# Output chunks of a fused mixture-of-experts and recurrence kernel: two halves of four consecutive steps in place of odd and even steps

## The chip, the cores and the metric

The kernel runs on one core of a Trainium2 chip. The metric is the device time in microseconds of one execution, as the median of several runs. Engines are named as in the profile: PE is the matrix engine (PEld its weight loads), DVE the vector engine, ACT the scalar engine, POOL the GpSimd engine, SP the engine that here only issues DMAs; SPq, PEq and so on are the instruction queues of these engines.

## The reference, cut to what matters

The input x is 32 sequences of 256 steps of 256 channels. First a mixture-of-experts layer is added to it (8192 tokens, a shared gated network and the two best of 8 experts each). Its result is called x again, and a recurrence over the 256 steps is added:

```
x = x + moe(x, cond)
def step(h, z_t):
    gate = sigmoid(h @ Wh.T + z_t @ Wz.T + b)
    h_new = tanh(h * (1 - alpha) + gate * z_t)
    return h_new, h_new
out = x + scan(step, cond, x over the 256 steps)
```

So each output value is one element of the recurrence's input plus the state of that step. The states follow one another: step s needs the state of step s-1.

## The kernel before, in words

All work of the mixture layer is cut into 170 numbered units (152 of experts and of the shared network, then 18 drain units), each a fixed sequence of PE instructions with numbered gaps between them. The recurrence runs beside it: one step is 12 small matmuls on PE (`gate_high`, `gate_step`), a tanh on ACT (`act_gate`, L1241), two DVE operations (`rec_pre`: `taken` L1542, `pre` L1545), two tanh on ACT (`act_h`: `hs_high` L1249, `hist` L1250) and two more DVE operations (`rec_low`: `hs_low` L1551, and `kept` L1534 for the step after). In which gap of which unit each piece of a step stands is written out by hand in the tables `PE_AT`, `ACT_AT` and `DVE_AT`; every engine runs its instructions strictly in that order, with semaphores between the engines.

On chip the channels are on the 128 partitions, in two halves (`KC = 2`), and within a partition the steps and the 32 sequences (`NB = 32`) follow one another. `zq` holds the recurrence's input halved, `hist` the states of the last 24 steps, both with the 32 sequences contiguous and the steps 64 elements apart.

The output leaves in 32 chunks of 8 steps (`HALF = 8`), at the units of the table `OUT_AT` (46 to 156). A chunk goes through four engines:

- `out_channels(c)` on DVE (L1565) computes 2 * zq + hist for 8 steps and 32 sequences, 256 elements per partition, once for each of the two channel halves, into the tile `o_ch` (64 instructions in all). Between the two there is a gap in which pieces of recurrence steps may stand.
- PE (L1922), one unit later, turns `o_ch` with four transposes of 128 x 128 into the PSUM bank `spare`: two token groups of 128 tokens, two channel halves.
- ACT (`act_out`, L1184) copies the bank to `o_tok`, of which there are two. Chunk c may overwrite what chunk c-2 used once its store has landed (L1183).
- SP (`store`, L958-959) waits for the copy and issues one DMA of 256 KB to the output in DRAM.

The 8 steps are numbered t * 2 + j. A token group is one j: group 0 has the even steps, group 1 the odd ones, and a partition of `o_tok` is one (sequence, t) and holds the rows of both j, which are neighbours in DRAM, so each partition is stored as one run of 2 KB. For that, `o_ch` is laid out as (j, sequence, t) with t innermost, four values:

```
out_v = out.rearrange("b (a t j) c -> a b t (j c)", t=TT, j=2)            # L532
o_ch[:, kc].rearrange("p j b t -> p t j b")                               # L1565, the output
```

The inner loop of the DVE instruction runs over the 32 sequences, and so writes with a stride of four elements (16 bytes); both of its inputs are read in runs of 32 neighbouring elements.

SP issues in program order, unit by unit (`body`): the load of the residual, the transposing loads of token pairs for the experts (`load_pair`, L948), the stores of expert results (`store_pair`, L967), transposing loads of tokens (`turn_x`, L928) and plain ones (`load_x`, L912), then the output store of that unit (L959), and last, at section borders, the first loads of the next section (`first_pairs`). At the very end it waits until all stores have landed (L1018-1019). The expert results stored by SP are read back by indirect DMAs of POOL (L1121) and summed on DVE (`gated`, L1506 and L1510).

Of the kernel before, what the change touches and what calls it, by code (L numbers as in the profile page):

```python
# [13 lines left out]
P = 128  # L14
# [484 lines left out]
def moe_gated_recurrence(nc, x, cond, router_w, router_b, w1, w3, w2, w1e, w2e, gate_w, gate_b, alpha, out):  # L499
    NB, T, C = x.shape  # L500
    E, _, HE = w1e.shape
    HS = w1.shape[1]
    KC = C // P
    TT = P // NB
# [3 lines left out]
    HALF = TG // 2  # L508
# [4 lines left out]
    NSTEP = T  # L513
# [15 lines left out]
    x_slots = [nc.dram_tensor(f"x_slots_{n}", [NT * P, 2 * C], F16).ap() for n in ("even", "odd")]  # L529
    y_slots = [nc.dram_tensor(f"y_slots_{n}", [NT * P, C], F32).ap() for n in ("even", "odd")]  # L530
    x_in = x.rearrange("b (q t j) c -> q b t (j c)", t=TT, j=GROUP)
    out_v = out.rearrange("b (a t j) c -> a b t (j c)", t=TT, j=2)  # L532

    with ExitStack() as ctx:
        def sb(name, shape, dt=F32):
            return ctx.enter_context(nc.sbuf_tensor(name, shape, dt))

        def sem(name):
            return ctx.enter_context(nc.semaphore(name))
# [112 lines left out]
        hist = sb("hist", [P, TS, KC, NB])  # L652
        hs = [sb(f"hs_{h}", [P, 2, KC, NB], F16) for h in HL]
        th = sb("th", [P, 2, KC, NB])
        pre = sb("pre", [P, 2, KC, NB])
        o_ch = sb("o_ch", [P, KC, 2, NB, TT])
        o_tok = sb("o_tok", [P, 2, 2, C])


# [70 lines left out]
        s_out = [sem(f"s_out{i}") for i in range(4)]  # L730
# [17 lines left out]
        def released(eng, what, part):  # L748

            at = SPARE.index((what, part))  # L750
            if at == 0:
                return
            what, part = SPARE[at - 1]
            if what == OUT:
                eng.wait_ge(s_otok, part + 1)
            elif what == LOGITS:
                eng.wait_ge(s_lg, part + 1)
            elif what == SUM:
                eng.wait_ge(s_z, part[0] * KC + part[1] + 1)
            else:  # L760
                eng.wait_ge(s_rk, part + 1)

        def turned(eng, q):

            if q < N_TURN:
                eng.wait_ge(s_xslo, KC * (q + 1))
            else:
                eng.wait_ge(s_xs[q % NXP], len(range(q, N_TURN - 1, -NXP)) * (16 * GROUP))
# [82 lines left out]
        def conv_parts(key):  # L851

            kind, i = key
            if kind == "w1e":
                k, m = divmod(i, 2)
                src = w1e[:, k * P:(k + 1) * P, m * P:(m + 1) * P].rearrange("e p h -> p e h")
                return src, [w[k][m][:].rearrange("p e h -> p (e h)") for w in w1e_s], 1, E, P
            if kind == "w2e":
                k, part = divmod(i, 2)
                some = slice(part * (E // 2), (part + 1) * (E // 2))  # L860
                src = w2e[some, k * P:(k + 1) * P, :].rearrange("e p c -> p e c")
                return src, [w[k][:, some].rearrange("p e c -> p (e c)") for w in w2e_s], 1, E // 2, C
            if kind == "w13":
                src, dst = (w1, w3)[i].rearrange("(k p) h -> p k h", p=P), [w[:, i] for w in w13_s]
                return src, [d.rearrange("p k h -> p (k h)") for d in dst], 1, KC, HS
            src, dst = w2.rearrange("(k p) h -> p k h", p=P), [w[:, :, :] for w in w2_s]
            return src, [d.rearrange("p k h -> p (k h)") for d in dst], 1, MID, C
# [31 lines left out]
        def z_of(c):  # L899

            return zq[:, c // 2 % NZQ, (c % 2) * HALF:(c % 2 + 1) * HALF]
# [5 lines left out]
        def _(sp):  # L907
# [48 lines left out]

            def store(c):
                sp.wait_ge(s_otok, c + 1)  # L958
                sp.dma_start(out_v[c], o_tok[:, c % 2].rearrange("p j c -> p (j c)")).then_inc(s_out[c % 4], 16)  # L959

            def store_pair(u):

# [53 lines left out]
            for u in UNITS:  # L1016
                body(u)
            for part in range(4):  # L1018
                sp.wait_ge(s_out[part], 16 * (NSTEP // HALF // 4))


        @block.gpsimd
# [122 lines left out]
        def _(act):  # L1145
# [7 lines left out]
            for n in range(N_ACT_LOADS):  # L1153
                src, _, a, k, w = conv_parts(CONV[n])
# [24 lines left out]
            def act_out(c):  # L1179
                act.wait_ge(s_turno, c + 1)  # L1180

                if c >= 2:
                    act.wait_ge(s_out[(c - 2) % 4], ((c - 2) // 4 + 1) * 16)  # L1183
                nc.scalar.activation(o_tok[:, c % 2].rearrange("p j c -> p (j c)"),  # L1184
                                     spare[:], ACT.Copy).then_inc(s_otok, 1)

# [70 lines left out]
            def body(u):  # L1257
# [41 lines left out]
                if MISC.get(u.i, (None,))[0] == OUT:  # L1299
                    act_out(MISC[u.i][1])  # L1300
# [50 lines left out]
        def _(dve):  # L1351
# [204 lines left out]
            def out_channels(c, gap):  # L1556

                dve.wait_ge(s_h, (c + 1) * HALF + 1)
                if c > 0:
                    dve.wait_ge(s_turno, c)  # L1560
                some = slice(c * HALF % TS, c * HALF % TS + HALF)
                for kc in range(KC):
                    if kc > 0:
                        gap()
                    ins = dve.scalar_tensor_tensor(o_ch[:, kc].rearrange("p j b t -> p t j b"),  # L1565
                                                   z_of(c)[:, :, kc, :].rearrange("p (t j) b -> p t j b", j=2), 2.0,
                                                   hist[:, some, kc, :].rearrange("p (t j) b -> p t j b", j=2),
                                                   ALU.mult, ALU.add)
                ins.then_inc(s_och, 1)

# [126 lines left out]
            for t in range(TT):  # L1697
                ins = dve.tensor_copy(cond_t[:, :, :, t], bank[0][:, 0:COLS].rearrange("p (k b) -> p k b", k=KC))
# [20 lines left out]
        def _(pe):  # L1719
            PASSES = ((0, 0), (1, 0), (0, 1))  # L1720

            def mm(out_ap, w, mov, start, stop):
                return pe.matmul(out_ap, w, mov, start=start, stop=stop, skip_group_check=True)  # L1723

            def pairs(out_ap, w, mov, start, stop, chunks):


                last, n = None, len(chunks) * 3
                for i, k in enumerate(chunks):
                    for j, (a, c) in enumerate(((0, 0), (1, 0), (0, 1))):  # L1730
                        last = mm(out_ap, w(a, k), mov(c, k), start and i == 0 and j == 0, stop and i * 3 + j == n - 1)
                return last
# [117 lines left out]
            def sum_routed(q, kc, gap):  # L1850

                for j in range(GROUP):
                    if j > 0:
                        gap()
                    if kc == 0:
                        pe.wait_ge(s_r, q * GROUP + j + 1)
                    last = pe.transpose(spare[:, j * P:(j + 1) * P], r_sum[:, j, kc * P:(kc + 1) * P], ident[:])  # L1857
                last.then_inc(s_half if kc == 0 else s_y, 1)
# [36 lines left out]
            def misc(what, part, gap):  # L1895
                released(pe, what, part)
                if what == LOGITS:
                    for q in range(TILE0[part] // GROUP, TILE0[part + 1] // GROUP):
                        turned(pe, q)
                    for j in range(SECTIONS[part]):  # L1900
                        q, i = divmod(TILE0[part] + j, GROUP)
                        last = pairs(spare[:, j * E:(j + 1) * E],
                                     lambda a, k: xs[:, q % NXS, a, k, i * P:(i + 1) * P],
                                     lambda c, k: rwx[c][:, k, :], True, True, range(KC))
                    last.then_inc(s_lgps, 1)
                elif what == RANKS:
                    J = SECTIONS[part]
                    pe.wait_ge(s_route, part * N_ROUTE_LINKS + MASK_LINK)
                    chosen = mask16[:, 0:J].rearrange("p j e -> p (j e)")
                    mm(spare[:, 0:J * E], below[:], chosen, True, False)  # L1910
                    for d in range(1, J):
                        mm(spare[:, d * E:J * E], ones16[:], chosen[:, 0:(J - d) * E], False, False)
                    for j in range(J):
                        last = mm(spare[:, J * E:J * E + E], ones16[:], mask16[:, j, :], False, j == J - 1)
                    last.then_inc(s_rkps, 1)
                elif what == SUM:
                    sum_routed(*part, gap)
                else:
                    pe.wait_ge(s_och, part + 1)
                    for j in range(2):  # L1920
                        for kc in range(KC):
                            last = pe.transpose(spare[:, j * C + kc * P:j * C + (kc + 1) * P],  # L1922
                                                o_ch[:, kc, j].rearrange("p b t -> p (b t)"),
                                                ident[:])
                    last.then_inc(s_turno, 1)

# [109 lines left out]
```

## Time and profile before

| | before |
|---|---|
| median of 3 runs | 783.67 us (783.11 to 784.78) |
| profiled execution | 779.37 us |
| its span, first to last instruction | 777.3 us |
| mean granted TensorE clock | 0.959 |
| PE busy | 714.0 us, 92% |
| DVE busy | 548.3 us, 71% |
| ACT busy | 472.2 us, 61% |
| DMA packets | 167106, 124.83 MB |

The profiled execution is one run with the hardware profiler on. Its span leaves out 2.1 us of start and end that its own time has. Busy is the time in which an engine works on an instruction; the chain that ended last is followed back from the last instruction, at each step to what released it. A granted clock of 1.0 is the full clock of PE, 0.5 half of it. In the windows below, the number in brackets behind a busy time is the count of instructions; the last three are the granted clock, the mean busy share of the DMA engines, and the GB/s they moved.

### The profile page before, as it was taken

How to read it: one execution, taken by the hardware profiler on the slowest of the kernel's cores; microseconds unless marked ns; L12 is line 12 of the kernel's file. 1: busy time of each engine (PE TensorE's matmuls, PEld its weight loads, DVE VectorE, ACT ScalarE, POOL GpSimd, SP SyncE). 2: the span in 40 equal slices, each digit the busy share in tenths (PEclk: the TensorE clock that was granted, in tenths of full speed). 3: DMA queues.
4: the chain of work that ended last, by engine and by line, in shares of the span. 5: the costliest groups of instructions: out<-in, count | busy, mean ns of one | idle time of the engine just before them, and what ended most of it. 6: DMA issues, size and time to landing. Idle time of an engine off the chain costs nothing.

```text
span 777.3 us, 23838 instructions
## 1 busy us (share of the span) xinstructions
PE 714.0 (92%) x8562; PEld 513.2 (66%) x8562; DVE 548.3 (71%) x2014; ACT 472.2 (61%) x1347; POOL 269.7 (35%) x284
## 2 busy tenths in 40 slices
PE   5899998988999899999989999999999999999763
PEld 3455486544888656898658887566888655686442
DVE  4887651437877498876658987798885678866754
ACT  4745574624677565667647676565877645676533
POOL 2037365155642056453066015774030073002100
PEclk9999999989999999999989999999999999999865
DMA  8836799683896767887949854456476355123101
GB/s 287 312 115 230 211 232 284 170 198 106 199 252 160 172 114 190 184 207 168 189 142 217 173 125 157 137 164 144 104 180 162 103 145 141 43 89 117 43 14 42
DMA packets 167106, 124.83 MB, mean 161 GB/s; under 512 B 119346, under 2 KB 147796, under 8 KB 166996
## 3 DMA queue, kind: packets, MB, share of 16 engines
q1 hardware_dynamic: 151076, 79.20, 42.7%
q0 software_dynamic: 14368, 41.96, 18.2%
q10 hardware_dynamic: 1552, 2.15, 0.8%
q8 instruction: 76, 1.25, 0.7%
q14 instruction: 34, 0.28, 0.1%
HBM read 39.90 MB, written 55.84 MB: 123 GB/s over the span
## 4 chain that ended last, share of the span: by engine, by line
PE 70%; DVE 13%; ACT 6%; DMA 4%; issue 3%; SPq 2%; DVEq 0%; ACTq 0%; POOL 0%; POOLq 0%
PE bank L1723 66%; PE bank L1922 2%; PE bank L1857 2%; SPq L928 2%; DVE hid_low L1491 1%; DVE pre L1545 1%; DMA xe<-x_slots_even 1%; DVE full L1484 1%; DVE taken L1542 1%; ACT th L1241 1%; ACT hs_high L1249 1%; DMA xs<-x_parts 1%; DVE r_part L1506 1%; DVE r_sum L1510 1%; DVE o_ch L1565 1%
## 5 line engine op out<-in xcount | busy, mean ns | idle before, releaser
L1723 PE MATMUL bank<-xe,w1e_high 128*128 128x128 f16 x1360 | 216.8, 221 | 5.9 <-DMA xe<-x_slots_even 3.9
L1723 PE MATMUL bank<-xs,w_high 128*128 128x512 f16 x512 | 169.4, 386 | 5.0 <-DVE w_low L1661 2.8
L1723 PE MATMUL bank<-xe,w1e_low 128*128 128x128 f16 x680 | 147.8, 220 | 0.0
L1491 DVE TENSOR_TENSOR hid_low<-full,hid_high 128x512 f16<-128x512 f32 (+1 forms) x152 | 103.0, 677 | 46.6 <-ACT hid_high L1194 36.6
L1723 PEld LDWEIGHTS bank<-xe,w1e_high 128*128 x1360 | 115.3, 98 | 26.3 <-issue 13.8
L1241 ACT ACTIVATE th<-bank 128x64 f32<-128x64 f32 x256 | 56.9, 222 | 104.6 <-PE bank L1723 100.5
L1542 DVE SCALAR_TENSOR_TENSOR taken<-th,zq 128x64 f32<-128x64 f32 x256 | 57.8, 226 | 79.9 <-ACT th L1241 75.8
L1249 ACT ACTIVATE hs_high<-pre 128x64 f16<-128x64 f32 x256 | 65.5, 256 | 72.2 <-DVE pre L1545 63.3
L1723 PEld LDWEIGHTS bank<-hs_high,gwt_high 128*128 128x128 f16 x1024 | 70.1, 97 | 49.5 <-ACT hs_high L1249 34.3
L1062 POOL TENSOR_TENSOR fence_pool<-zero 128x1 f32<-128x1 f32 x12 | 2.9, 245 | 282.2 <-DMA y_slots_odd<-y_pair 88.4
L1723 PE MATMUL bank<-xs,w_low 128*128 128x512 f16 x256 | 98.8, 386 | 0.0
L1723 PE MATMUL bank<-hs_high,gwt_high 128*128 128x32 f16 x1024 | 79.0, 178 | 20.3 <-ACT hs_high L1249 20.0
L1723 PE MATMUL bank<-w2e_high,hid_high 128*128 x340 | 93.2, 274 | 0.4 <-ACT y_pair L1203 0.3
L1723 PE MATMUL bank<-w2e_low,hid_high 128*128 x340 | 92.5, 272 | 0.0
L1723 PE MATMUL bank<-w2e_high,hid_low 128*128 x340 | 92.2, 271 | 0.0
L1103 POOL DMA_INDIRECT x_slots_even<-x_parts,where x72 | 76.2, 1059 | 44.4 <-PE bank L1723 32.9
L1723 PEld LDWEIGHTS bank<-xs,w_high 128*128 128x128 f16 x512 | 49.7, 99 | 57.8 <-issue 10.1
L1121 POOL DMA_INDIRECT y_got<-y_slots_even,where x72 | 72.2, 1003 | 39.1 <-PE bank L1723 22.1
L1551 DVE TENSOR_TENSOR hs_low<-hist,hs_high 128x64 f16<-128x64 f32 x256 | 56.6, 221 | 37.2 <-ACT hist L1250 34.8
L1723 PE MATMUL bank<-hs_high,gwt_low 128*128 128x32 f16 x1024 | 77.6, 177 | 0.0
L1103 POOL DMA_INDIRECT x_slots_odd<-x_parts,where x56 | 57.0, 1018 | 48.9 <-PE bank L1723 41.8
L1723 PE MATMUL bank<-hs_low,gwt_high 128*128 128x32 f16 x1024 | 66.2, 179 | 5.2 <-DVE hs_low L1551 4.0
(156 smaller groups left out, 1709.3 us busy)
## 6 DMA issues: line engine op xcount, KB each, us to landing
y_slots_even<-y_pair SPq DMA_DIRECT2D x45, 256.0 KB
y_slots_odd<-y_pair SPq DMA_DIRECT2D x37, 256.0 KB
x_res<-in_x_dram SPq DMA_DIRECT2D x16, 512.0 KB
out_dram<-o_tok SPq DMA_DIRECT2D x32, 256.0 KB, 3.1
x_tok<-in_x_dram SPq DMA_DIRECT2D x14, 512.0 KB, 4.5
x_slots_even<-zeros POOLq DMA_DIRECT2D x1, 4096.0 KB, 17.9
x_slots_odd<-zeros POOLq DMA_DIRECT2D x1, 4096.0 KB, 15.2
y_got<-in_L_cond_W1e_dram SPq DMA_DIRECT2D x4, 512.0 KB, 11.2
```

The source lines that it names most:

```text
L928: sp.dma_start_transpose(xs[:, q % NXS].rearrange("p h k s -> p (h k) s")[:, :, j * P:(j + 1) * P], halves(q)[:, j].rearrange("p h c -> p ...
L1103: pool.indirect_dma_start(x_slots[n % 2], at_slots(n, j, k), halves(q)[:, i].rearrange("p h c -> p (h c)"), None).then_inc(s_scat[n % 2], 16)
L1121: pool.indirect_dma_start(y_got[:, tile % NYG, k, :], None, y_slots[n % 2][0:(2 * PAIRS[n] - 1) * P, :], at_slots(n, j, k)).then_inc(s_got ...
L1241: nc.scalar.activation(flat3(th[:, s % 2]), gate_sums(s), ACT.Tanh, scale=0.5 / UP).then_inc(s_th, 1)
L1249: nc.scalar.activation(flat3(hs[0][:, s % 2]), src, ACT.Tanh).then_inc(s_hhi, 1)
L1484: dve.scalar_tensor_tensor(buf, buf, 1.0 / UP, shared_bank(u, 1)[:], ALU.mult, ALU.mult).then_inc(s_prod, 1)
L1491: dve.tensor_tensor(hid[1][:, u.i % NR, some], full32[:, u.i % 2, some], hid[0][:, u.i % NR, some], ALU.subtract).then_inc(s_lo, 1)
L1542: dve.scalar_tensor_tensor(flat3(taken[:, s % 2]), flat3(th[:, s % 2]), 1.0, flat3(z_of(s // HALF)[:, s % HALF]), ALU.add, ALU.mult).then_ ...
L1551: dve.tensor_tensor(flat3(hs[1][:, s % 2]), flat3(hist[:, s % TS]), flat3(hs[0][:, s % 2]), ALU.subtract).then_inc(s_hlo, 1)
L1723: return pe.matmul(out_ap, w, mov, start=start, stop=stop, skip_group_check=True)
L1857: last = pe.transpose(spare[:, j * P:(j + 1) * P], r_sum[:, j, kc * P:(kc + 1) * P], ident[:])
L1922: last = pe.transpose(spare[:, j * C + kc * P:j * C + (kc + 1) * P], o_ch[:, kc, j].rearrange("p b t -> p (b t)"), ident[:])
```

## The change

An output chunk keeps its 8 steps, but they are split as first four, last four, not as even and odd. `o_ch` becomes (step, sequence), so the sum is written without a stride, and with plain contiguous runs; the four transposes read halves of it, in which a partition of the result is one (t, sequence). A partition of `o_tok` then has two rows that are four steps apart, so each half is stored by a DMA of its own, 128 KB, each partition one run of 1 KB. The semaphores of the stores count 32 for a chunk where they counted 16. The order tables are untouched.

```diff
-    out_v = out.rearrange("b (a t j) c -> a b t (j c)", t=TT, j=2)
+    out_v = out.rearrange("b (a t) c -> a t b c", t=TT)
...
-        o_ch = sb("o_ch", [P, KC, 2, NB, TT])
+        o_ch = sb("o_ch", [P, KC, HALF, NB])
...
             def store(c):
                 sp.wait_ge(s_otok, c + 1)
-                sp.dma_start(out_v[c], o_tok[:, c % 2].rearrange("p j c -> p (j c)")).then_inc(s_out[c % 4], 16)
+                for j in range(2):
+                    sp.dma_start(out_v[2 * c + j], o_tok[:, c % 2, j]).then_inc(s_out[c % 4], 16)
...
             for part in range(4):
-                sp.wait_ge(s_out[part], 16 * (NSTEP // HALF // 4))
+                sp.wait_ge(s_out[part], 32 * (NSTEP // HALF // 4))
...
                 if c >= 2:
-                    act.wait_ge(s_out[(c - 2) % 4], ((c - 2) // 4 + 1) * 16)
+                    act.wait_ge(s_out[(c - 2) % 4], ((c - 2) // 4 + 1) * 32)
...
-                    ins = dve.scalar_tensor_tensor(o_ch[:, kc].rearrange("p j b t -> p t j b"),
-                                                   z_of(c)[:, :, kc, :].rearrange("p (t j) b -> p t j b", j=2), 2.0,
-                                                   hist[:, some, kc, :].rearrange("p (t j) b -> p t j b", j=2),
+                    ins = dve.scalar_tensor_tensor(o_ch[:, kc], z_of(c)[:, :, kc, :], 2.0, hist[:, some, kc, :],
                                                    ALU.mult, ALU.add)
...
                             last = pe.transpose(spare[:, j * C + kc * P:j * C + (kc + 1) * P],
-                                                o_ch[:, kc, j].rearrange("p b t -> p (b t)"),
+                                                o_ch[:, kc, j * TT:(j + 1) * TT].rearrange("p t b -> p (t b)"),
                                                 ident[:])
```

## Rows read from the trace of the kernel before

**Rows 1.** Windows: stretch, length, busy us of PE, PEld, DVE, ACT, POOL, clock, DMA.
```profile
222.00:745.00 523.00, 503.63 (x6595) 375.65 (x6593) 396.67 (x1504) 341.07 (x1075) 172.36 (x179) 0.98 0.60 145
745.00:777.30 32.30, 13.39 (x191) 9.39 (x190) 14.79 (x65) 11.38 (x49) 0.00 (x0) 0.60 0.09 34
```

**Rows 2.** Waits of PE, 222 to 745 us: total us, times, longest.
```profile
PE bank L1723 <- ACT hs_high L1249: 7.3, 10, 1.3
PE bank L1723 <- DVE hs_low L1551: 4.0, 5, 2.8
...
PE bank L1922 <- DVE o_ch L1565: 0.4, 1, 0.4
```

**Rows 3.** Page, part 4: the chain that ended last, shares of the span.
```profile
PE 70%; DVE 13%; ACT 6%; DMA 4%; issue 3%; SPq 2%; DVEq 0%; ACTq 0%; POOL 0%; POOLq 0%
```

**Rows 4.** The chain in order of time: start us, length us, what.
```profile
292.24 0.40 DVE r_sum L1510
...
293.24 1.01 DVE o_ch L1565 x2
...
750.09 0.52 DVE o_ch L1565
```

**Rows 5.** DVE groups by shape: count, busy us, mean ns, idle before.
```profile
L1491 DVE TENSOR_TENSOR hid_low<-full,hid_high 128x256 f16<-128x256 f32 x6 | 2.5, 420 | 0.4 <-ACT hid_high L1194 0.4
L1506 DVE SCALAR_TENSOR_TENSOR r_part<-y_got,gate,x_res 128x256 f32<-128x256 f32 x64 | 30.5, 477 | 3.4 <-DMA y_got<-y_slots_even,where 3.4
L1524 DVE SCALAR_TENSOR_TENSOR zq<-bank,zq 128x512 f32<-128x512 f32 x32 | 21.9, 684 | 2.4 <-PE bank L1857 2.2
L1565 DVE SCALAR_TENSOR_TENSOR o_ch<-zq,hist 128x256 f32<-128x256 f32 x64 | 38.5, 620 | 0.5 <-ACT hist L1250 0.5
L1698 DVE COPY cond_t<-bank 128x64 f32<-128x64 f32 x4 | 0.7, 261 | 1.8 <-PE bank L1995 1.8
L1473 DVE COPY ranks<-bank 128x104 f32<-128x104 f32 x5 | 1.3, 258 | 0.0
L1473 DVE COPY ranks<-bank 128x40 f32<-128x40 f32 x1 | 0.2, 190 | 0.0
```

**Rows 6.** The output store's line: issue ns min/median/max, then landing.
```profile
L959 SPq DMA_DIRECT2D out_dram<-o_tok x32: 539/605/1508, 228.4 to 774.4; - x32
DMA to landing us min/median/max: 2.3/3.1/4.5
```

**Rows 7.** Timeline of SP around 380 us, merged: start, length.
```profile
379.44 0.61 SPq L959 DMA_DIRECT2D out_dram<-o_tok  x1
380.14 6.45 SPq L948 DMA_TRANSPOSE xe<-x_slots_odd  x4
```

**Rows 8.** The chain in the same stretch, in order of time.
```profile
383.07 0.72 SPq L948
...
385.29 1.30 SPq L948
...
387.27 4.16 DMA y_slots_even<-y_pair
```

**Rows 9.** The chain's end, in order of time.
```profile
771.49 0.61 DVE o_ch L1565
772.70 1.10 PE bank L1922 x4
...
773.83 0.60 ACT o_tok L1184
```

**Rows 10.** Timeline of SP at the end: start, length.
```profile
774.45 0.54 SPq L959 DMA_DIRECT2D out_dram<-o_tok  x1
```

**Rows 11.** Waits of SP's queue, 774 us to the end: total us, times, longest.
```profile
SPq L1019 <- DMA out_dram<-o_tok: 1.7, 1, 1.7
```

**Rows 12.** DMA view, 774 us to the end: rates in 40 slices, then all packets.
```profile
GB/s 0 0 0 0 0 0 0 0 0 0 0 0 0 0 0 0 0 0 0 25 273 472 447 397 422 397 397 273 75 0 0 0 0 0 0 0 0 0 0 0
DMA packets 144, 0.26 MB, mean 79 GB/s; under 512 B 16, under 2 KB 16, under 8 KB 144
```

## The prediction

> **What bounds the kernel now.** I read the windows first, then what PE waits for, then the chain, then the groups of DVE by shape. From 222 us, when the first chunk leaves, to 745 us PE is busy 503.6 of 523 us [rows 1]: the reader is to see that nothing that shortens another engine can win more than the 19.4 us that are left, and that DVE at 396.7 us has much slack on average. What PE waits for by name in there is small: 7.3 us for `hs_high`, 4.0 us for `hs_low`, both steps of the recurrence, and 0.4 us for `o_ch` itself [rows 2]. After 745 us only the recurrence is left: PE busy 13.4 of 32.3 us, at a mean granted clock of 0.60, so a part of the time at 1.2 GHz [rows 1]. There the loop PE, ACT, DVE, ACT sets the time. The chain is PE for 70% of the span, DVE for 13%, SP's queue for 2% [rows 3], so both engines that the change touches do stand on it, in places.
>
> **The sum on DVE.** The stride is what the change removes, so what does it cost? L1565 takes 620 ns for 256 elements [rows 5]. Two other two-input operations on 256 elements are contiguous at the output: `hid_low` 420 ns, which writes fp16, and `r_part`, which reads a scalar per partition as well, 477 ns. A second estimate is of the stride alone: L1698 is a copy of 64 elements from PSUM which writes with this same stride of four floats, 261 ns; the copies L1473 of 40 and 104 elements without it take 190 and 258 ns, so 64 elements would take 190 + 24/64 * 68 = 215 ns. The stride costs 46 ns for 64 elements, or 0.7 ns each, 180 ns for 256. That brings 620 to 440 ns, between the two. Reading with a stride is not the cost: L1524 reads PSUM with a stride of four floats and writes runs of 32, and takes 684 ns for 512 elements. I take 420 ns, because `hid_low` has no scalar operand and neither has L1565; the bounds are 620 (no gain) and 420, and 477 lies between. In the chain, where each piece ends when the next instruction starts, `r_sum` holds DVE for 0.40 us and a pair of `o_ch` for 1.01 us [rows 4]; a pair at 420 ns is about 0.6 to 0.7 us. So each of the 64 instructions frees 0.20 us, 12.8 us of DVE's busy time.
>
> The Trainium skill speaks against this gain: its page "SBUF — State Buffer", section "Door 1: The DMA port swizzle", says that SBUF is reached in lines of 16 bytes, that an access to a new line pays, and that fp32 can be strided by 4 for free. The stride here is 4, so by that limit L1565 would stay at 620 ns and the sum would be the third rival's. The trace differs, with the 0.7 ns an element above.
>
> **What of it lies on the path.** 12.8 us less of DVE is not 12.8 us of time. On the chain before the last chunk I count eight pieces of `o_ch` with nine instructions in all, of which rows 4 show the first, a pair at 293.24, and the last, at 750.09. That last one gives nothing: the tanh that the next DVE operation needs is itself only just done. That leaves eight instructions, 8 * 0.20 = 1.6 us, if nothing else comes in their place. But PE has the next claim: in these stretches it is nearly full and its own order is fixed, and the named wait for `o_ch` is 0.4 us in all [rows 2]. I take half, 0.8 us, with 0 and 1.6 as bounds. For the other 50 or so instructions PE's work is the cover; were the cover gone, they would be worth at most 0.2 us each.
>
> **The tail.** The last chunk stands wholly on the chain: the pair starts at 771.49, PE's transposes at 772.70, ACT's copy at 773.83 [rows 9], SP's issue at 774.45 [rows 10]. The pair is 0.4 us shorter (0.28 at 477 ns, 0 if the stride is free). Transposes and copy have the same shapes as before: nothing.
>
> **The stores.** Each chunk has one DMA issue more on SP. An issue takes 0.605 us at the median, 0.54 at least [rows 6]. In all 32 * 0.6 = 19 us of SP's queue, and most of it beside SP's waits for ACT, PE and DVE. The packets cost little: of a run of 2 KB two of 1 KB are made, 4096 packets more, of the same bytes.
>
> Behind the store in the queue stand the loads of token pairs. One place is on the chain: the store at 379.44 has four loads behind it [rows 7], the third of which waits on PE and goes at 383.07, then an expert store lands after 4.16 us [rows 8], and POOL's gather and DVE's sum wait for that. Two loads at about 1.3 us each [rows 8] after 380.14 are out by 382.74, so 0.33 us before 383.07. A second issue of 0.65 us uses that up and makes this stretch 0.32 us later, if the gather's delay reaches PE. I take 0.3 us; bounds 0 and 0.65. The wait for `o_tok` on chunk c-2 (L1183) asks for a landing of 3.1 us, 4.5 at most [rows 6], of a store several units back: nothing. The thresholds of 32 need both halves, which follow each other by one issue.
>
> At the end, SP issues at 774.45 for 0.54 us and waits 1.7 us more for the landing [rows 10, 11]. The data moves in nine of 40 slices of 3.3 us, 0.75 us for 0.26 MB [rows 12], so a half takes 0.37 us. After the change the first half leaves with the same first issue; the second is issued 0.54 + 0.05 us later and lands its 0.37 us of data behind that. 0.59 + 0.37 - 0.75 = 0.2 us later than before. The trace shows no output store of 128 KB; if an issue has the 0.605 us median and the landing does not shrink with the size, it is 0.65 us later; if the second issue is cheaper than the first, 0. I take 0.2.
>
> **The sum**, against the profiled execution's own 779.37 us: - 0.8 (middle) - 0.4 (last pair) + 0.3 (SP at 380 us) + 0.2 (last landing) = - 0.7 us, so 778.7 us. The median of the runs shown is 783.67, 4.3 us above that execution; I take the difference over unchanged: 783.67 - 0.7 = 783.0 us. The bounds of the terms give - 0.4 - 1.6 = - 2.0 us, and + 0.65 + 0.65 = + 1.3 us.
>
> **Rivals.**
> First, more than the chain shows: the recurrence runs ahead. A shorter `o_ch` lets every step behind it finish earlier, and PE's waits for `hs_high` and `hs_low`, 11.3 us in the middle [rows 2], shrink. For it speaks that the tables put pieces of steps right behind `o_ch`; against it, that PE waits on these in 15 places only, while there are 32 chunks, and that the gaps' order is fixed, so a step that is ready early waits for its gap. If a third of these waits goes, 3.8 us, with the last pair 4.2 us, less the 0.5 of the stores: 780.0 us. Half of that effect already leaves my band: 781.9 us.
>
> Second, the stores cost more than the sum gives: slower. The mechanism is SP's queue: with the transposing loads at 1.3 us each and issues at 0.6 us, a section's start is a train without gaps, and 0.65 us put into it moves every load behind. It decides from the point where the slack ahead of SP's next wait is under 0.65 us; at 380 us it is 0.33. The price is 0.65 us for each train that a store meets; if four of the 32 chunks meet one on PE's path, 2.6 us, and with 0.65 at the end and 0.4 won by the last pair: + 2.85 us, 786.5 us; with two, 785.2. Against it speaks that SP's queue has 2% of the chain [rows 3], and most of that before the first store.
>
> Third, the change does not do what it says: L1565 stays near 620 ns since the cost is in reading two SBUF inputs in runs of 32 elements, and not in writing. Then only the stores' + 0.5 us are left, 784.2 us, 1.2 us more at most. L1698 speaks against it. This is where the Trainium skill's limit, cited above from "SBUF — State Buffer", would lead.
>
> **How the numbers follow.** What a measurement of this kernel can tell from no change is about 0.2%, 1.6 us: faster is below 782.1, slower above 785.2. My forecast, 783.0 us, has a chance of 50%, the recurrence that runs ahead 22%, the queue 20%, the stride that costs nothing 8%. Of the forecast 5 points are faster and 45 the same; of the first rival 20 and 2; of the second 16 points are slower and 4 the same; the 8 are the same. That is 0.25 faster, 0.59 same, 0.16 slower. The forecast alone ranges from 781.7 to 785.0 us. The range for 8 in 10 reaches towards both other cases: 780.6 to 785.9 us.
>
> **What would show it.** L1565 at 400 to 480 ns, with DVE's busy time 9 to 13 us lower; 64 issues of L959 and 4096 packets more, and some 500 of 4 bytes for semaphores; `taken` and `hs_low` behind a lone `o_ch` start 0.2 us earlier but PE's waits in the middle stay within 1 us of 11.7; the last pair to the transposes 0.8 us in place of 1.21; the last landing wait about as now but behind a second issue. It would be wrong if L1565 stays above 550 ns, if PE's idle time in the middle falls by more than 2 us, or if the waits for DMAs of `xe` or `y_got` grow by more than 1 us.

## The result, and the profile after

The change makes the kernel slower: 789.71 us (787.38 to 792.86, 9 runs) against 783.11 us (778.91 to 786.75, 9 runs) for the kernel before, a ratio of 1.0096 with a 95% interval of 1.007 to 1.0123 (the ratio compares all runs of the two kernels; their two medians alone give 1.0084). The forecast was 783.0 us, 0.1% under the 783.67 us that were known for the kernel before, with a range up to 785.9 us. The profiled execution took 789.71 us, its span is 787.9 us, 10.6 us more than before.

The groups of DVE by shape come first, as in rows 5: count, busy us, mean ns, idle before.

```profile
L1507 DVE SCALAR_TENSOR_TENSOR r_part<-y_got,gate,x_res 128x256 f32<-128x256 f32 x64 | 30.6, 479 | 8.3 <-DMA y_got<-y_slots_even,where 7.0 <-issue 1.3
L1566 DVE SCALAR_TENSOR_TENSOR o_ch<-zq,hist 128x256 f32<-128x256 f32 x64 | 26.3, 420 | 0.5 <-ACT hist L1251 0.5
```

The sum does what it was to do: 420 ns in place of 620 [rows 5]. But the other row has changed too: `r_part` waits 7.0 us for gathered expert results, where it waited 3.4 [rows 5]. The time did not go to DVE's work.

The windows of the same two stretches, as in rows 1:

```profile
222.00:745.00 523.00, 497.75 (x6502) 370.36 (x6500) 382.36 (x1480) 337.75 (x1061) 174.22 (x178) 0.98 0.66 145
745.00:787.90 42.90, 19.93 (x260) 14.16 (x260) 19.34 (x86) 14.75 (x62) 0.00 (x0) 0.59 0.08 25
```

In the middle PE is busy 5.9 us less in the same 523 us, so it waits more, at the same clock. The mean busy share of the 16 DMA engines is 0.66 and was 0.60, while they move the same 145 GB/s [rows 1]. The DMA engines are busy longer for the same bytes: that is the first sign.

PE's waits from 222 to 745 us, as in rows 2:

```profile
PE bank L1722 <- ACT hs_high L1250: 7.7, 9, 1.3
PE bank L1722 <- DVE hs_low L1552: 6.6, 5, 5.5
PE bank L1722 <- issue: 4.0, 7, 1.4
```

The wait of 5.5 us ends at 400.65 us. It is the wait that was the longest in rows 2 too, with 2.8 us. The chain before it, in order of time (start us, length us), and SP's timeline (start, length, merged) say what grew:

```profile
388.37 2.11 SPq L948
...
391.29 3.44 DMA y_slots_even<-y_pair
...
396.97 2.87 DMA y_got<-y_slots_even,where
...
399.97 0.48 DVE r_part L1507
400.45 0.15 DVE hs_low L1552
```

```profile
379.95 1.25 SPq L960 DMA_DIRECT2D out_dram<-o_tok  x2
381.32 9.16 SPq L948 DMA_TRANSPOSE xe<-x_slots_odd  x4
```

This is the place that the prediction looked at in rows 7 and 8. The four transposing loads behind the output stores now hold SP's queue for 9.16 us, not 6.45 [rows 7]. So the expert store behind them leaves later, POOL's gather behind that one too, DVE stands in `r_part`, and the recurrence's `hs_low` is behind `r_part` on DVE. The two landings in this chain did not grow: 3.44 us for the expert store, which took 4.16 [rows 8], and 2.87 us for the gather.

The chain also has a gather that lands 8.73 us after its issue at 413.51 us. It is not shown to be the stores' doing: SP issues no output store between 394.89 and 454.7 us.

Further on, the chain again:

```profile
584.63 0.58 SPq L960
...
585.25 6.14 DMA out_dram<-o_tok
...
591.48 0.07 ACT o_tok L1185
```

An output store now lands 6.14 us after its issue (3.1 at the median, 4.5 at most before [rows 6]), and ACT's copy two chunks later waits 1.5 us for it; in before no such wait shows. SP's timeline of the same time (start, length, merged) shows its other side:

```profile
584.63 1.16 SPq L960 DMA_DIRECT2D out_dram<-o_tok  x2
585.84 2.72 SPq L948 DMA_TRANSPOSE xe<-x_slots_even  x1
588.61 0.59 SPq L968 DMA_DIRECT2D y_slots_even<-y_pair  x1
589.25 2.88 SPq L960 DMA_DIRECT2D out_dram<-o_tok  x2
592.17 2.73 SPq L948 DMA_TRANSPOSE xe<-x_slots_even  x1
```

The first two issues take 1.16 us together, but each transposing load behind a pair takes 2.7 us to issue. The kernel before, at the same place:

```profile
579.60 0.58 SPq L959 DMA_DIRECT2D out_dram<-o_tok  x1
580.22 1.41 SPq L948 DMA_TRANSPOSE xe<-x_slots_even  x1
```

Over the kernel the loads for odd sections take 1.94 us at the median; before, it was 1.37 (the line's own rows, issue ns as min/median/max; the first of after, the second of before). For even sections it is 1.43 against 1.31 us.

```profile
L948 SPq DMA_TRANSPOSE xe<-x_slots_odd x40: 1197/1939/4127, 156.5 to 698.1; - x40
```

```profile
L948 SPq DMA_TRANSPOSE xe<-x_slots_odd x40: 1198/1366/4076, 159.0 to 689.1; - x40
```

What is wrong with the store is best seen where it is alone, at the end. The DMA view of the last 5.5 us (busy share of the 16 engines in tenths and GB/s, both in 40 slices, then all packets), and SP's last wait, as in rows 12 and 11:

```profile
DMA  0000000000122112322232222222222220000000
GB/s 0 0 0 0 0 0 0 0 0 0 37 37 22 15 37 89 112 89 97 89 112 89 97 89 104 97 89 89 104 104 89 89 97 30 0 0 0 0 0 0
DMA packets 264, 0.26 MB, mean 48 GB/s; under 512 B 8, under 2 KB 264, under 8 KB 264
...
SPq L1020 <- DMA out_dram<-o_tok: 3.5, 1, 3.5
```

The same 0.26 MB move at some 95 GB/s and not at some 400 [rows 12], a quarter, and the busy share stays at 2 to 3 tenths, which is what four engines of sixteen give. And there are 8 packets under 512 bytes, of 4 bytes each, where one store alone had 16 [rows 12]. The reading is that a DMA ends with one such packet on each engine that it uses; then two DMAs with 8 between them use four engines each. The doses below test it. The page's count agrees: 170947 packets, 3841 more than before, and not the 4096 more of data plus 512 of 4 bytes that were forecast: 256 of 4 bytes have gone, which is what 64 stores on 4 engines have less than 32 on 16.

So the reading is that each half is stored by 4 of the 16 DMA engines. The kernel before stores with a DRAM side of [32 sequences][4 t][2 KB]; after, it is [4 t][32 sequences][1 KB]. The outermost dimension is 4.

### The profile page after: what moved, and what is told of

Read it like the earlier page. It is cut to its first block, busy times and chain, and to the rows that moved or that the text cites. A ratio compares the mean times of both kernels' runs of the same rounds, so it can differ in the third digit from the quotient of the medians.

```text
span 787.9 us, 23870 instructions
## 1 busy us (share of the span) xinstructions
PE 714.8 (91%) x8562; PEld 513.3 (65%) x8562; DVE 540.0 (69%) x2014; ACT 473.0 (60%) x1347; POOL 271.7 (34%) x284
## 2 busy tenths in 40 slices
DMA packets 170947, 124.84 MB, mean 158 GB/s; under 512 B 119090, under 2 KB 155732, under 8 KB 170836
## 4 chain that ended last, share of the span: by engine, by line
PE 67%; DVE 10%; DMA 7%; ACT 7%; issue 4%; SPq 3%; POOL 1%; ACTq 0%; DVEq 0%; POOLq 0%
PE bank L1722 63%; PE bank L1921 1%; DMA y_got<-y_slots_even,where 1%; PE bank L1856 1%; DMA xe<-x_slots_even 1%; SPq L948 1%; DMA x_slots_even<-x_parts,where 1%; SPq L928 1%; DVE pre L1546 1%; DVE taken L1543 1%; ACT th L1242 1%; POOL y_got L1122 1%; DVE hid_low L1492 1%; ACT hs_high L1250 1%; DMA xs<-x_parts 1%
## 5 line engine op out<-in xcount | busy, mean ns | idle before, releaser
L1122 POOL DMA_INDIRECT y_got<-y_slots_even,where x72 | 74.5, 1035 | 37.4 <-PE bank L1722 19.9
```

The lines of the kernel that those rows point to most:

```text
L1122: pool.indirect_dma_start(y_got[:, tile % NYG, k, :], None, y_slots[n % 2][0:(2 * PAIRS[n] - 1) * P, :], at_slots(n, j, k)).then_inc(s_got ...
```

## The experiments

Theory 1: a store whose outermost dimension is 4 runs on 4 engines, its packets pile up there, and what stands behind them (transposing loads, expert stores, gathers, the next output store) lands late. Theory 2: the second issue on SP's queue and the smaller packets cost, the prediction's slow rival. Theory 3: DVE's freed time upsets the order tables. The runs were made in groups, each with its own runs of the kernel before; so the time that a result is set against is 780.87, 780.52 or 784.25 us.

**One edit to the kernel before: the outermost dimension**, four_engines_alone.

```diff
-    out_v = out.rearrange("b (a t j) c -> a b t (j c)", t=TT, j=2)
+    out_v = out.rearrange("b (a t j) c -> a t b (j c)", t=TT, j=2)
```

> The kernel before, with the outermost dimension of the store's DRAM side made the 4 values of t and not the 32 sequences; still one DMA of 256 KB in runs of 2 KB for a chunk, the sum still strided (rows land at wrong places of the output). Theory 1, a store whose outermost dimension is 4 runs on 4 of the 16 DMA engines, and that is what costs: +5 to +8 us against before (790 at a before of 783), no packet of the last store on more than 4 engines, about 100 GB/s at the end in place of 400, the last landing wait 3 us or more in place of 1.7. Theory 2, the second issue on SP and the 1 KB packets cost: within 1.5 us of before. Theory 3, freed DVE time upsets the fixed order: within 1.5 us of before.

Measured: 796.65 us against 780.87, ratio 1.02 (1.0167 to 1.0233). One issue for a chunk, packets of 2 KB, the strided sum, and twice the loss of after. Its last 5.5 us:

```profile
DMA packets 132, 0.26 MB, mean 48 GB/s; under 512 B 4, under 2 KB 4, under 8 KB 132
...
SPq L1019 <- DMA out_dram<-o_tok: 5.1, 1, 5.1
```

Four packets of 4 bytes, four engines. Theory 1 holds, in direction; that it costs 15.8 us, where 5 to 8 were expected, and more than the two smaller stores below, was expected by none of the theories, and no run tells why.

**The sum alone**, sum_contig_only: after, with the store of before.

```diff
-    out_v = out.rearrange("b (a t) c -> a t b c", t=TT)
+    out_v = out.rearrange("b (a t j) c -> a b t (j c)", t=TT, j=2)
...
-                for j in range(2):
-                    sp.dma_start(out_v[2 * c + j], o_tok[:, c % 2, j]).then_inc(s_out[c % 4], 16)
+                sp.dma_start(out_v[c], o_tok[:, c % 2].rearrange("p j c -> p (j c)")).then_inc(s_out[c % 4], 16)
```

> The kernel after with the store of before: one DMA of 256 KB, 16 engines, runs of 2 KB (rows land at wrong places of the output). Only the contiguous sum is left of the change. Theories 1 and 2: before - 0.4 to - 1.6 us, as the prediction's terms for the middle and the last pair. Theory 3, freed DVE time upsets the fixed order of the engines: slower than before by 3 us or more.

Measured: 779.16 against 780.87 us, ratio 0.9974 (0.9952 to 0.9996): 2.0 us faster by the ratio, 1.7 by the medians, a little more than expected. Theory 3 is out. The 0.2 us that each of the 64 instructions gives back, 12.8 us of DVE, are worth 2.0 us.

**The stores alone**, after_stores_only: before, with the two stores of after (`out_v`, `store` and the counts of 32 as in the change's diff, nothing else of it).

> The kernel before with the two stores of after for a chunk (outermost dimension 4, runs of 1 KB, two issues; rows land at wrong places of the output); the sum still strided. Theory 1 and 2: as after or up to 1.6 us slower, +6.5 to +9 us against before. Theory 3: within 1.5 us of before.

Measured: 790.77 against 780.87 us, ratio 1.0127 (1.0094 to 1.0159), 9.9 us slower, just above the 6.5 to 9 expected. With the sum's - 0.26% that makes + 1.01%, and the whole change measured + 0.96%: the two parts add up.

**Two stores on all engines**, two_stores_16: before, with its chunk cut into even and odd steps.

```diff
-    out_v = out.rearrange("b (a t j) c -> a b t (j c)", t=TT, j=2)
+    out_v = out.rearrange("b (a t j) c -> a j b t c", t=TT, j=2)
...
-                sp.dma_start(out_v[c], o_tok[:, c % 2].rearrange("p j c -> p (j c)")).then_inc(s_out[c % 4], 16)
+                for j in range(2):
+                    sp.dma_start(out_v[c, j], o_tok[:, c % 2, j]).then_inc(s_out[c % 4], 16)
```

> The kernel before with two stores for a chunk, one for the even and one for the odd steps, each 128 KB in runs of 1 KB, outermost dimension the 32 sequences; right rows, strided sum. Theory 1: only the terms of the prediction, +0.2 to +1.3 us against before. Theory 2, the second issue on SP and the small packets cost: +5 us or more.

Measured: 781.1 against 780.87 us, ratio 1.0002 (0.9974 to 1.0029). Same two issues, same runs of 1 KB, same bytes as in after_stores_only, and no loss that can be measured: the interval is 2 us to either side. The loads for odd sections are back at 1.33 us at the median (1.90 in after_stores_only), the four at 378 us at 6.27 us in place of 9.16. Theory 2 is out as the cause of the 9.9 us. The last 5.5 us:

```profile
GB/s 0 0 0 0 0 0 0 0 0 0 0 0 0 0 0 0 0 0 0 0 0 0 0 0 0 37 313 387 209 8 119 350 380 105 0 0 0 0 0 0
DMA packets 288, 0.26 MB, mean 48 GB/s; under 512 B 32, under 2 KB 288, under 8 KB 288
...
SPq L1020 <- DMA out_dram<-o_tok: 1.4, 1, 1.4
```

The reader is to see two humps of some 380 GB/s with a gap, the second issue, and 32 packets of 4 bytes, 16 for each store. This is what the prediction had in mind for the tail.

**The dose**, two_stores_8 and two_stores_2: the same two stores with an outermost dimension of 8 or of 2.

```diff
+    out_v = out.rearrange("(j b) (a s) c -> a j s b c", j=2, s=HALF)        # two_stores_8
+    out_v = out.rearrange("a (j s h) c -> a j h s c", j=2, h=2)             # two_stores_2
```

> The kernel before with two stores for a chunk, 128 partitions in runs of 1 KB, outermost dimension 8 (rows land at wrong places of the output); strided sum. Same issues, packets and bytes as two_stores_16 (outermost 32, +0.0 %) and after_stores_only (outermost 4, +1.27 %). Theory 1: 8 engines at the end, about 200 GB/s, and a time between those two, near the first: +0.1 to +0.6 % against before. Rival, only the scatter of the rows in DRAM costs and not the number of engines: the rows of a run of packets are as far apart as in after_stores_only, so +1.0 % or more.

> As two_stores_8, with outermost dimension 2 and 64 rows under it (rows land at wrong places, all of a chunk in one sequence's 256 KB, so close together). Theory 1: two engines, about 50 GB/s at the end, a last landing wait of 6 us or more, and slower than after_stores_only by 1.5 % or more, +3 % or more against before. Rival, the scatter of the rows costs: near before, under +0.5 %.

Measured: two_stores_8 783.44 against 780.52 us, ratio 1.0037 (1.0018 to 1.0056); two_stores_2 821.3 us, ratio 1.0519 (1.0475 to 1.0563). The last 5.5 us of the one and of the other:

```profile
DMA  0000000000000000000145345545555410000000
GB/s 0 0 0 0 0 0 0 0 0 0 0 0 0 0 0 0 0 0 0 45 82 67 60 149 194 186 171 179 186 171 194 171 37 15 0 0 0 0 0 0
DMA packets 272, 0.26 MB, mean 48 GB/s; under 512 B 16, under 2 KB 272, under 8 KB 272
...
SPq L1020 <- DMA out_dram<-o_tok: 2.2, 1, 2.2
```

```profile
GB/s 22 22 37 7 45 52 52 45 45 52 52 45 45 45 60 45 45 45 60 45 45 45 60 45 45 45 60 45 45 45 60 45 45 22 0 0 0 0 0 0
DMA packets 207, 0.21 MB, mean 38 GB/s; under 512 B 4, under 2 KB 207, under 8 KB 207
...
SPq L1020 <- DMA out_dram<-o_tok: 6.5, 1, 6.5
```

| outermost dimension | kernel | 4-byte packets of two stores | rate at the end | last wait | ratio to before |
|---|---|---|---|---|---|
| 32 | two_stores_16 | 32 | up to 387 GB/s | 1.4 us | 1.0002 |
| 8 | two_stores_8 | 16 | some 180 GB/s | 2.2 us | 1.0037 |
| 4 | after_stores_only | 8 | some 95 GB/s | 3.6 us | 1.0127 |
| 2 | two_stores_2 | 4 | some 48 GB/s | 6.5 us | 1.0519 |

From row to row the rate and the count of packets halve. If half the packets is the number of engines, 16, 8, 4 and 2, each engine moves 22 to 24 GB/s in all four rows. The rows of two_stores_2 lie close together in DRAM and those of two_stores_8 far apart, so the scatter of the rows is not the cause. The loss grows faster than the engines fall away.

The Trainium skill states this in "DMA: Bandwidth & Descriptors", section "Why a DMA increments its semaphore by 16 and not by 1": a DMA takes as many engines, up to 16, as divide the slowest dimension of both of its sides, and, for a DMA like SP's, the lowest-numbered ones. The four rates above agree with its first half; which engines they are, these views don't show. The prediction had not drawn on it.

**The change's own layout on all engines**, four_stores_16: after, with one store for each t.

```diff
-    out_v = out.rearrange("b (a t) c -> a t b c", t=TT)
+    out_v = out.rearrange("b (a j t) c -> a t b j c", t=TT, j=2)
...
-                for j in range(2):
-                    sp.dma_start(out_v[2 * c + j], o_tok[:, c % 2, j]).then_inc(s_out[c % 4], 16)
+                for t in range(TT):
+                    sp.dma_start(out_v[c, t], o_tok[t * NB:(t + 1) * NB, c % 2]).then_inc(s_out[c % 4], 16)
```

> The kernel after, right output, with four stores for a chunk in place of two: one for each t, 32 partitions of two runs of 1 KB, outermost dimension the 32 sequences. Two issues more on SP than after, four times those of before. Theory 1, the engines: in spite of the issues 5 us or more faster than after, -1 to +3 us against before (the contiguous sum's - 2.0 us, three issues more in each chunk), the last data at some 400 GB/s. Theory 2, issues on SP cost: as after or slower, +7 us or more against before.

Measured: 779.09 against 780.52 us, ratio 0.9983 (0.9956 to 1.0011). With two issues more than after for each chunk it is 1.1% faster than after (0.9983 to 1.0096). By its ratio it beats both kernels; against before that is not beyond its interval. One expectation failed: the last data came in humps of up to 216 GB/s, not at some 400. Its 64 packets of 4 bytes are 16 for each store, so the engines are all in use; why a store of 64 KB from 32 partitions moves no faster is not shown. The last wait is 1.2 us all the same. An issue is shorter too, 439 ns at the median against 552 in after:

```profile
L960 SPq DMA_DIRECT2D out_dram<-o_tok x128: 315/439/2466, 226.3 to 772.1; - x128
```

**Eight engines and the stride moved to PE**, parity_8: the contiguous sum, and token groups of 8 steps by 16 sequences.

```diff
+    out_v = out.rearrange("(b j) (a s) c -> a j s b c", j=2, s=HALF)
...
-                                                o_ch[:, kc, j * TT:(j + 1) * TT].rearrange("p t b -> p (t b)"),
+                                                o_ch[:, kc].rearrange("p s (b j) -> p j (s b)", j=2)[:, j],
```

> Right output. The contiguous sum of after, but PE's transposes read every second element (stride two floats), so a token group is 8 steps of 16 sequences and each of the two stores has the outermost dimension 8. Theory 1: 8 engines; the cost of two_stores_8 less the 2.0 us of the contiguous sum, -0.3 to +0.4 % against before, and 4 us or more faster than after. If PE's weight load pays for the stride, L1922's loads are over 140 ns.

Measured: 783.52 against 780.52 us, ratio 1.0044 (1.0024 to 1.0063), just above the range expected. Against the 1.0037 of two_stores_8 the sum's 2.0 us are not seen to come back, though the two intervals could hide most of them. One thing that may take from them is PE's weight load with a stride of two floats, 209 ns at the median where it was 140 in after; what it costs by itself no run shows:

```profile
L1921 PEld LDWEIGHTS bank<-ident,o_ch x128: 194/209/230, 224.5 to 778.0; 128*128 128x128 f32 x128
```

**Where in the run the loss arises**, middle_16 and last_16: after, with the stores of four_stores_16 for chunks 0 to 27, or for the last one only (the counts waited for follow). Theory 1a is that most of the loss is in the middle, theory 1b that it is at the end.

```diff
+    spread = [c < 28 for c in range(NSTEP // HALF)]         # middle_16; last_16 has c == 31
...
+                for t in range(TT) if spread[c] else ():
+                    sp.dma_start(out_16[c, t], o_tok[t * NB:(t + 1) * NB, c % 2]).then_inc(s_out[c % 4], 16)
+                for j in range(2) if not spread[c] else ():
```

> The kernel after, right output, with the four 16-engine stores of four_stores_16 for chunks 0 to 27 and the two 4-engine stores for the last four chunks, which leave after the last expert work. Theory 1a, most of the loss is in the middle, where loads and expert stores stand behind output packets on the first four engines: 5 us or more faster than after, and slower than four_stores_16 by the last landing alone, 1.5 to 3 us, so 0 to +0.3 % against before. Theory 1b, most of the loss is at the end: within 2 us of after.

> The kernel after, right output, with the four 16-engine stores for the last chunk only. Theory 1a: faster than after by the end alone, 1 to 2.5 us, so +0.6 to +0.9 % against before. Theory 1b: near before, under +0.3 %. The last wait is near 1.7 us again in place of 3.5, behind three issues in place of one.

Measured: middle_16 783.99 against 784.25 us, ratio 0.9995 (0.9972 to 1.0017); last_16 788.29 us, ratio 1.0055 (1.0026 to 1.0083). Against the 1.0096 of after, the middle gives back 1.0%, the end 0.4%, and together a little more than the 1.1% between after and four_stores_16, within the intervals. Both kernels are just under what was expected. Theory 1a holds: most of the loss is in the middle.

The traces say where. The table has the time between the starts of the same tanh (`th`, L1241 in before), by its step counted from 0, and from the last of them to the end of the span; then PE's longest wait for `hs_low` and ACT's wait for an output store, all in us of the profiled executions.

| kernel | engines for a store | step 8 to 40 | 168 to 192 | 255 to the end | PE for `hs_low` | ACT for a store |
|---|---|---|---|---|---|---|
| before | 16 | 77.1 | 67.6 | 7.0 | 2.8 | none |
| two_stores_16 | 16 | 76.9 | 67.6 | 7.4 | 3.8 | none |
| four_stores_16 | 16 | 77.3 | 67.5 | 7.4 | 3.7 | none |
| two_stores_8 | 8 | 77.4 | 67.6 | 8.2 | 3.2 | none |
| middle_16 | 16, then 4 | 77.8 | 67.7 | 9.1 | 4.0 | none |
| last_16 | 4, then 16 | 78.9 | 70.8 | 7.5 | 5.4 | 1.4 |
| after | 4 | 79.5 | 70.8 | 9.1 | 5.5 | 1.5 |
| two_stores_2 | 2 | 85.8 | 73.9 | 12.3 | 8.6 | 3.9 |

So the loss arises at a few places and not evenly, and each place follows the engines that its own stores use: steps 8 to 40, where the first output stores leave, the section border at 380 us, steps 168 to 192 with the late landing at 585 us, and the end. Not all of a trace's loss is the stores': from step 80 to 104 after takes 66.0 us where before takes 62.5, but two_stores_16 takes 65.6 and middle_16 68.8 there.

## Why the prediction was wrong, by its own steps

- **The sum on DVE** was right: 420 ns forecast and measured. The Trainium skill's limit of four fp32 for a free stride ("SBUF — State Buffer", "Door 1: The DMA port swizzle") does not hold for this write: 620 ns against 420 for the same work. DVE's total fell from 548.3 to 540.0 us, by 8.3 us, just under the 9 to 13 that were to be seen.
- **The path and the last pair**: - 1.2 us forecast, bounds - 2.0 and 0; - 2.0 us measured by sum_contig_only, with 0.3 to 3.7 us by its interval. Right in kind and near the far bound. The pair now starts at 779.98 and PE at 780.89, 0.91 us after (0.8 forecast, 1.21 before [rows 9]):

```profile
779.98 0.43 DVE o_ch L1566
...
780.89 1.10 PE bank L1921 x4
```

- **The second issue and the smaller packets**: + 0.5 us forecast (0.3 at 380 us and 0.2 at the end), 0.0% measured when the stores run on all engines (two_stores_16), with 2 us to either side. So they are small, as forecast; whether 0.5 is right, the runs can't tell. In the trace of two_stores_16 the end, from the first of SP's last output issues, is 3.20 us long, where before had 2.85.
- **The step that failed** stands in the part on the stores: "so a half takes 0.37 us", and with it "the packets cost little" and the landing of "a store several units back: nothing". All three take for granted that a half-store spreads over 16 engines as the store before did. Only the size of the runs and the number of issues were read from the diff, not the order of the dimensions. A half takes about 1.4 us at 95 GB/s, an estimate from the 0.13 MB that it moves, not 0.37. The end from the first of SP's last output issues is 5.23 us long in place of 2.85: + 2.4 us where + 0.2 was forecast. A landing of 6.14 us reaches ACT's copy. And at 380 us, where + 0.3 was forecast, the four loads take 2.7 us longer and PE's wait grows by 2.7 us; with sixteen engines and the same issues it grows by 1.0.
- **The rivals**: the slow one had the right side and the right neighbours (SP's train of loads), but the wrong cause. With four trains and the end its stores cost 3.25 us, which is beyond the interval of two_stores_16; with two they cost 1.95 us, which is not. The sum of its figures, 785.2 to 786.5 us, is not near enough to save it.
- **The signs to look for** were well chosen: the wait for `y_got` grew by 3.6 us and PE's idle time in the middle by 5.9, and growth of the first was named as what would refute the prediction. The missing packets of 4 bytes name the cause.
- **The sum made anew**: - 2.0 (contiguous sum) + 9.9 (stores on four engines, after_stores_only) = + 7.9 us; the ratio of 1.0096 is + 7.5 us.

## What to carry to other kernels

When a change reorders the rows of a DMA, read the outermost dimension of both sides before anything else: if it is 8, 4 or 2, the DMA runs on that few engines here, and what SP issues behind it goes out later. Where the layout forces a small outermost dimension, more DMAs with a large one are cheaper than few with a small one: here four issues beat two. Count the 4-byte packets of a lone DMA in the trace: in these runs they told how many engines it used.

## What the runs showed of the hardware that was not expected

- The cost of few engines is not in proportion: two stores a chunk on 16, 8, 4, 2 engines for the same 8 MB of output gave ratios of 1.0002, 1.0037, 1.0127, 1.0519.
- One DMA of 256 KB on four engines costs more (1.02) than two of 128 KB on four engines (1.0127). This stays open.
- A transposing load's issue on SP stretches from 1.3 to 2.7 us behind two stores on four engines, and stays at 1.3 behind two on sixteen (two_stores_16 at 583 us): the queue of issues is held back as well, not only the landing.
- A strided write of fp32 in steps of 16 bytes costs DVE 200 ns for 256 elements, and a stride of 8 bytes costs PE's weight load 69 ns for 128 columns.
